# A graph network's second edge sort, run in one stage with the first layer's weighted sum and node update

## What is computed

```python
attn = attn_exp / (attn_sum[row] + 1e-08)
out = jax.ops.segment_sum(attn[:, :, None] * v[col], row, num_segments=n)
out = out.reshape(n, HID) @ Wo.T + bo
h = x + out
return layernorm(h) * ln_g + ln_b            # and then x = layernorm(x + that)
```

## Time and profile before

| | |
|---|---|
| median of 3 runs | 9654.35 us (9615.33 to 14809.4) |
| profiled execution, its own time | 9625.82 us |
| span of the profiled execution | 9624.1 us |
| sum0, from the softmax's end to the last addition | 2739 to 3056 us |
| update0 | 3056 to 3170 us |
| second sort | 3170 to 4351 us |
| POOL busy over the span | 6249.1 us (65%) |

### The profile page before, as it was taken

One profiled execution on the slowest core, in us unless ns is written; L12 is line 12 of the kernel. 1 busy time (PEld: TensorE's weight loads), 2 busy tenths in 40 slices (PEclk: granted clock), 3 DMA queues, 4 the chain that ended last, 5 costly groups with the idle time before them and its releaser, 6 DMA issues. The chain is left out here.

```text
span 9624.1 us, 137530 instructions
## 1 busy us (share of the span) xinstructions
PE 5695.4 (59%) x35183; PEld 5161.4 (54%) x35183; DVE 5182.6 (54%) x14594; ACT 2020.1 (21%) x3984; POOL 6249.1 (65%) x6325
## 2 busy tenths in 40 slices
PE   6777747777566576663777753777743333433334
PEld 5666637777545566663666643666633333333333
DVE  7666634444577655552777762444454444344445
ACT  0111111111156111111444432444430000000000
POOL 2777737777454577773777724777717777577774
PEclk9555568888778555557899975555555555655556
DMA  0000027777434000004555514334302111211111
GB/s 8 2 2 2 2 67 200 210 210 210 133 120 122 9 2 2 2 2 123 136 135 135 135 47 64 78 79 79 79 19 57 52 52 52 56 50 52 52 53 47
DMA packets 842488, 705.60 MB, mean 73 GB/s; under 512 B 308280, under 2 KB 733758, under 8 KB 841846
## 3 DMA queue, kind: packets, MB, share of 16 engines
q0 software_dynamic: 211680, 354.89, 15.2%
q1 hardware_dynamic: 499960, 286.30, 11.6%
q10 hardware_dynamic: 130584, 61.48, 2.2%
HBM read 608.13 MB, written 93.92 MB: 73 GB/s over the span
## 5 line engine op out<-in xcount | busy, mean ns | idle before, releaser
L1224 PE MATMUL sum_ps_sum<-sum_hot,sum_msg 128*128 128x128 f32 x3528 | 841.2, 431 | 1433.5 <-DVE acc L1193 1293.1
L1224 PEld LDWEIGHTS sum_ps_sum<-sum_hot,sum_msg 128*128 128x128 f32 x3528 | 770.5, 330 | 1504.3 <-DVE acc L1193 1348.1
L1292 POOL DMA_INDIRECT attend_rows<-h_table,dst_other x882 | 879.1, 997 | 521.5 <-issue 267.7
L1168 POOL DMA_INDIRECT sum_rows<-x_table,dst_other x882 | 845.5, 959 | 475.7 <-issue 268.5
L440 POOL DMA_INDIRECT payload_dst<-load_dst_pay_slot,load_dst_at_i x882 | 862.5, 978 | 440.4 <-issue 262.4
L440 POOL DMA_INDIRECT payload_src<-load_src_pay_slot,load_src_at_i x882 | 862.4, 978 | 438.1 <-issue 275.9
L1292 POOL DMA_INDIRECT attend_rows<-xl_table,dst_other x882 | 883.6, 1002 | 392.9 <-issue 268.6
L869 POOL DMA_INDIRECT scores_rows<-kv_table,scores_idx x882 | 833.7, 945 | 416.5 <-issue 254.7
L1168 POOL DMA_INDIRECT sum_rows<-conv_table,dst_other x882 | 843.8, 957 | 349.4 <-issue 268.5
L1364 PE MATMUL attend_ps_sum<-attend_hot,attend_msg 128*128 128x128 f32 x3528 | 669.2, 365 | 496.4 <-DVE acc L1525 496.4
L1364 PEld LDWEIGHTS attend_ps_sum<-attend_hot,attend_msg 128*128 128x128 f32 x3528 | 615.7, 270 | 540.4 <-issue 467.2
(11 more groups left out here) (461 smaller groups left out, 14731.6 us busy)
## 6 DMA issues: line engine op xcount, KB each, us to landing
attend_win<-xr_table SPq DMA_DIRECT2D x882, 68.0 KB
scores_win<-q_table ACTq DMA_DIRECT2D x882, 64.0 KB
spill<-scores_rows SPq DMA_DIRECT2D x126, 448.0 KB
sum_rows<-spill SPq DMA_DIRECT2D x126, 448.0 KB
attend_rel_all<-rel_flat_dst SPq DMA_DIRECT2D x252, 224.0 KB
payload_src<-load_src_pay_slot,load_src_at_i POOLq DMA_INDIRECT x882
scores_rows<-kv_table,scores_idx POOLq DMA_INDIRECT x882
payload_dst<-load_dst_pay_slot,load_dst_at_i POOLq DMA_INDIRECT x882
```

The costliest lines, as they stand in the source:

```text
L1168: pool.indirect_dma_start(rows[:, g % deep, j, :], None, table, bass.IndirectOffsetOnAxis(ap=o.other[:, t:t + 1].bitcast(U32), axis=0)).th ...
L1224: mm = pe.matmul(ps_sum[:, n, j, :], msg[:, n, j, :], hot[:, n, j, :], start=True, stop=True)
L1292: pool.indirect_dma_start(rows[:, g % RING, j, :], None, table, bass.IndirectOffsetOnAxis(ap=o.other[:, t:t + 1].bitcast(U32), axis=0)).th ...
```

## The change

The first sort keeps its code. The second sort, sum0 and update0 become one stage, `sort_and_sum`. What it does:

- It works in slots n = -1 to 129. In slot n, group n+1 is compared, spread and counted, group n is looked up, and group n-1 is placed.
- **Wide histograms.** The running table is no longer a chain through ACT. Seven matmuls (`tables`) write counts for all seven tiles at once into a table of 8 x 50 columns: tile j is added into all later columns, 350, 300, ... 50 wide. DVE adds the base once (`add_tables`), and PE does the seven look-ups in a row.
- **Ranks on ACT.** PE puts (key of the other edge, or 16384 more for later edges) in PSUM; ACT takes Square(key - own key) and then Relu(1 - that) with a running sum, tile by tile: 14 activations a group, and ACT also copies the turned one-hot out.
- **Ticks.** The 128 ticks of the weighted sum are spread over slots 3 to 97 (`LAST_SUM = 97`), one or two in each: 33 slots have two. A tick adds the last group's products to `acc`, multiplies the next rows by the weights, now on DVE, and makes the next one-hot. There is one accumulator and one PSUM tile `ps_sum` of 7 results (and `ps_d` has one buffer of 4 tiles). From slot 99 on, every second slot holds one block of the node update, which ends in slot 121.
- POOL does nothing in the stage but scatter. All 882 addresses and payloads have a place of their own, so POOL waits only for the group's addresses.
- The source order's per-edge buffers are freed before this stage. `rows_by_tile` follows as before.

The core of the new stage, the orders of the engines and what the steps wait for:

```diff
+        LAST_SUM = 97
+        n_slots = R + 4
+        ticks_by = lambda n: min(R + 2, max(0, (n - 2) * (R + 2) // (LAST_SUM - 2)))
+        sum_ticks = {n: [t - 1 for t in range(ticks_by(n - 1), ticks_by(n))] for n in range(-1, n_slots)}
+        norm_ticks = {LAST_SUM + 2 + 2 * m: m for m in range(blocks + 2)}
...
+            @block.gpsimd
+            def _(pool):
+                for t in range(T):
+                    if t % G == 0:
+                        pool.wait_ge(at_ready, t // G + 1)
+                    pool.indirect_dma_start(
+                        o.payload, bass.IndirectOffsetOnAxis(ap=at_i[:, t:t + 1].bitcast(U32), axis=0),
+                        pay[:, t, :], None).then_inc(scattered, 16)
...
+            @block.tensor
+            def _(pe):
+                def spread_keys(g):
+                    pe.wait_ge(row_in[g % 3], 16 * (g // 3 + 1))
+                    if g:
+                        pe.wait_ge(ranked, G * g)
+                    for g0, g1 in ((0, 4), (4, G)):
+                        out = ps_key[:, g0:g1, :]
+                        pe.matmul(out, c.ident_bf[:], per_tile(later_mask[:], g1 - g0), start=True, stop=False)
+                        mm = pe.matmul(out, two_ones[:], row2[:, g % 3, g0 * P:g1 * P].rearrange("k (g e) -> k g e", e=P),
+                                       start=False, stop=True)
...
+                def turn_low(g):
+                    pe.wait_ge(compared, 2 * (g + 1))
...
+                        mm = pe.transpose(ps_lo_t[:, j, :], lo3[:, g % 3, :, j], c.ident_bf[:])
...
+                def tables(g):
+                    if g:
+                        pe.wait_ge(tabled, g)
...
+                    for j in range(G):
+                        later = ps_tab[:, (j + 1) * HB:(G + 1) * HB].rearrange("p (n h) -> p n h", h=HB)
+                        mm = pe.matmul(later, lo3[:, g % 3, :, j],
+                                       hi3[:, g % 3, :, j].rearrange("p (o h) -> p o h", o=1).to_broadcast([P, G - j, HB]),
+                                       start=(j == 0), stop=True, skip_group_check=True)
+                    mm.then_inc(tallied, 1)
...
+                def fill(w, half):
...
+                    if w or half:
+                        pe.wait_ge(squared, 2 * w + half)
...
+                def sums(w):
+                    pe.wait_ge(hot_ready, w + 1)
+                    pe.wait_ge(msg_ready, w + 1)
+                    pe.wait_ge(added, 1 + G * w)
+                    for j in range(G):
+                        mm = pe.matmul(ps_sum[:, j, :], msg[:, w % 2, j, :], hot[:, w % 2, j, :], start=True, stop=True)
+                    mm.then_inc(summed, 1)
...
+                def sum_tick(t):
+                    if t + 1 < R:
+                        fill(t + 1, 0)
+                    if 0 <= t < R:
+                        sums(t)
+                    if t + 1 < R:
+                        fill(t + 1, 1)
...
+                for n in range(-1, n_slots):
+                    ticks = sum_ticks[n]
+                    if ticks:
+                        sum_tick(ticks[0])
+                    if n + 1 < R:
+                        spread_keys(n + 1)
+                        turn_low(n + 1)
+                    for t in ticks[1:]:
+                        sum_tick(t)
+                    if 0 <= n < R:
+                        look_up(n)
+                    if n + 1 < R:
+                        tables(n + 1)
...
+            @block.scalar
+            def _(act):
+                def ranks(g):
+                    act.wait_ge(keys_spread, g + 1)
...
+                    for j in range(G):
+                        t = g * G + j
+                        act.activation(same[:, j, :], ps_key[:, j, :], ACT.Square,
+                                       bias=minus_key[:, t:t + 1]).then_inc(squares, 1)
+                    act.wait_ge(squares, G * (g + 1))
+                    for j in range(G):
+                        act.activation(same[:, j, :], same[:, j, :], ACT.Relu, bias=c.ones[:, 0:1], scale=-1.0,
+                                       accum_out=rank[:, g % 3, j:j + 1]).then_inc(ranked, 1)
...
+                for n in range(-1, n_slots):
+                    ticks = sum_ticks[n]
+                    for t in ticks[:1]:
+                        if t + 1 < R:
+                            one_hot(t + 1)
+                    if n + 1 < R:
+                        low_back(n + 1)
+                        ranks(n + 1)
+                    for t in ticks[1:]:
+                        if t + 1 < R:
+                            one_hot(t + 1)
...
+            @block.vector
+            def _(dve):
...
+                def add_tables(g):
+                    dve.wait_ge(tallied, g + 1)
...
+                def additions(w):
...
+                    dve.wait_ge(summed, w + 1)
+                    for j in range(G):
+                        dve.wait_ge(added, 1 + w * G + j)
+                        to = acc[:, bass.ds(base[j], P)]
+                        dve.tensor_tensor(to, to, ps_sum[:, j, :], ALU.add).then_inc(added, 1)
+
+                def sum_tick(t):
+                    if 0 <= t - 1 < R:
+                        additions(t - 1)
+                    if t + 1 < R:
+                        message(t + 1)
...
+                for n in range(-1, n_slots):
+                    ticks = sum_ticks[n]
+                    if 0 <= n < R:
+                        add_tables(n)
+                    if 0 <= n - 1 < R:
+                        place(n - 1)
+                    for t in ticks[:1]:
+                        sum_tick(t)
+                    if 2 <= n + 2 < R:
+                        compare(n + 2)
+                    for t in ticks[1:]:
+                        sum_tick(t)
+                    if n in norm_ticks:
+                        norm_tick(norm_ticks[n])
...
@@ gnn_kernel
-            weighted_sum(nc, c, by_src, "sum0", acc, scores, H0, spill=spill)
-            node_update(nc, c, "update0", acc, x, "attend",
-                        {"w": wo_t[:], "b": bo[:], "g": ln_g[:], "be": ln_b[:]})
-
-        sort_edges(nc, c, by_dst, dst, src, edge_weight, real, dst_counts, True)
+            sort_and_sum(nc, c, by_dst, dst, src, edge_weight, real, dst_counts, by_src, scores, spill, acc, x,
+                         {"w": wo_t[:], "b": bo[:], "g": ln_g[:], "be": ln_b[:]})
+        rows_by_tile(nc, c, by_dst)
```

More of the change, by code:

```diff
@@ L125, with __init__ @@
 class Order:
-    def __init__(self, nc, name, keep, by_tile):
+    def __init__(self, nc, name, keep, edges, by_tile):
         self.name, self.by_tile = name, by_tile
@@ L230, in sort_edges @@
         totals = st.sb("totals", [P, HB])
-        if count_next is not None:
+        if True:
             next_lo, next_hi = st.sb("next_lo", [P, T], BF16), st.sb("next_hi", [P, T], BF16)
@@ L257, in _ @@
                 act.wait_ge(paid, 4)
-                if not counted_before:
+                if True:
                     act.wait_ge(counted, 1)
@@ L2051, in gnn_kernel @@
         dram = lambda n, s: nc.dram_tensor(n, s, F32).ap()
-        by_dst = Order(nc, "dst", keep, True)
+        by_dst = Order(nc, "dst", keep, keep, True)
         c = constants(nc, keep)
@@ L2088, in gnn_kernel @@
-            segment_softmax(nc, c, by_src, "softmax0", scores, H0,
-                            {"real": by_src.real[:], "cut": cut[:], "be2": be2}, acc)
-            weighted_sum(nc, c, by_src, "sum0", acc, scores, H0, spill=spill)
-            node_update(nc, c, "update0", acc, x, "attend",
-                        {"w": wo_t[:], "b": bo[:], "g": ln_g[:], "be": ln_b[:]})
-        sort_edges(nc, c, by_dst, dst, src, edge_weight, real, dst_counts, True)
+            wo_t, bo, ln_g, ln_b = (lsb(n, [P, D]) for n in ("wo_t", "bo", "ln_g", "ln_b"))
```

326 lines of the change are left out of this document (294 added, 32 removed).

## The result

The changed kernel takes 10,202.6 us (median; 10,199.5 to 10,207.0), the kernel before beside it 9658.7 us: a ratio of 1.058 (95% interval 1.054 to 1.061); one of the four executions of the kernel before, a slow one of 14,809 us, is left out of the ratio. It is slower, as forecast, but by twice the amount: 9900 was expected, and 10,203 lies just outside the range that ended at 10,150.

What follows compares the result with a forecast made beforehand. Old sort bound by POOL's issue, new ticked slots by DVE and PE taking turns: 53 + 1555 + 256 + 19 = 1883 us against 1612, +271 on 9625.8, say 9900 us; range 9600 to 10,150.

Steps and rivals of the forecast that it cites:

- The loop between DVE and PE: Joint stage's ticked slots: DVE's first part and PE's whole slot take turns; one-tick slot 13.7 us.
- Rival 1: Joint stage: the loop doesn't bind, POOL's scatters do; 425 us less, 9200 us; chance 0.10.
- DVE's part: Each ticked slot: placing, table addition, register loads and seven additions on one accumulator; 5.7 us.
- PE's part: Each ticked slot: sums, look-up, spreading, turning, tables, half a fill; 6.0 us at 2.4 GHz, 10.85 at 1.2 GHz.
- The clock: PE's burst in each slot starts at 1.2 GHz and rises 5 us in; together 7.9 us.
- rival 3: Joint stage: the clock never rises; slots 16.5 and 23.5 us, +515 us, 10,140 us; chance 0.16.
- Slots with two ticks: 33 of 95 slots: PE's second fill waits for ACT's square behind the ranks; 21.4 us each.
- Head and tail: Joint stage outside the ticked slots: 53 us to slot 3; behind slot 97, 256 us bound by POOL, then 19.
- Rival 4: Joint stage: DVE's two-input operations block POOL's issue, 0.2 us each, 41 us in all; 9940 us; chance 0.05.
- Rival 2: Joint stage: the loop binds, the clock stays high; slots 11.7 and 17.4 us, +15 us, 9640 us; chance 0.26.
- A rounding: Old second sort: 882 scatters at 1.26 us of POOL's issue, given as a floor of 1113 us.

Runs made afterwards that it cites:

- c3: Changed kernel with no weighted sum before the sort has ended, sums and then node update in slots behind it; 10,048 us, scatters 1155 us.
- e6: Changed kernel in its own order, with the one-hot high parts laid out tile by tile so the tables' streamed columns lie side by side; 9986 us, ratio 1.036.
- c1: The changed kernel as it is, repeated as the control; 10,191 us, scatters 2120 us.
- c4: Changed kernel with ScalarE's ranks behind both one-hot tiles of a slot; 10,087 us, ratio 1.046.
- e7: Changed kernel with TensorE's sort work ahead of its sums, sums over 113 slots, an update step in each later slot, high parts by tile; 9345 us.
- e4: The same kernel as c3, sort first and sums behind it, run on a slower chip; 12,589 us, scatters 1388 us.

## Why the prediction was right in its sign and short in its size

- *The loop between DVE and PE*: right. PE waits for `acc` once a slot, DVE for the tables once a slot, and the order alone, changed, gives 615 us back. Rival 1 (POOL binds) fell for the kernel as written, and c3 shows that it holds for the sort without the sums.
- *DVE's part, 5.7 us*: right, 5.7 measured: 2.78 from `add_tables` to the first addition, with 0.85 of idle time for the register loads in it (0.8), and 2.81 for seven additions (2.75).
- *PE's part*: `sums` 3.33, `look_up` 3.2, `turn_low` 0.95 and the fills as forecast or within 0.15. `spread_keys` took 1.94 at half clock (3511.01 to 3512.95) for 1.5. **`tables` took 2.38 for 1.4 at half and 2.36 for 0.8 at the full clock.** This is one of the two steps that failed: I had priced columns, 1400 of them, and not where they lie. e6 with the columns side by side has 1.37 and 0.79, my two numbers.
- *The clock*: the other step that failed. I let every burst turn to the full clock 5 us in. Some do (in c1 after 4.4 us), but in 44 of the 62 single slots the clock stayed at half to the end, and 43 slots took 17.5 us or more (in c1 3517.27 to 3534.75), which is rival 3's 16.5 and the 1.0 of the tables. The 17 slots in which the clock rose took 15.2 to 15.6, and the 1.5 that they lie above the forecast of 13.7 is the tables at the full clock (2.36 for 0.8). With 16.7 on average the single slots cost 62 x 3.0 = 186 us more than forecast, about half of it the tables and half the clock.
- *Slots with two ticks*: right in the mechanism (PE waits 2.31 us for a square behind the ranks; c4 takes it away), 23.8 us for 21.4. The ranks took 4.66 us (3514.74 to 3519.4; Squares 0.25 to 0.26 from start to start, Relu and read 0.39) for 4.2, the tables 1.0 more; the rest, 0.9, is put down to the clock, in 14 of the 33 at half throughout. 33 x 2.4 = 79 us.
- *Head and tail*: 63 us for 53, and 306 for 275. Behind slot 97 POOL was not quite the bound: the starts of line 764 lie 10.0 us apart, where I had 8.83 and POOL's own pace in c3 is 9.17. That is 10 of the 31 us; for the rest POOL waited, while the update's steps and the placing were in DVE's one queue.
- Sum: 186 + 79 + 10 + 31 = 306 us, and 303 were missed. Rival 4 is there but small: a scatter takes 1042 ns on average in the changed kernel, 984 in c3 and 978 before (862.5 / 882), 56 us in all, most of it where POOL idles anyway.
- *Rival 2 and 3*: the clock went to rival 3's side; its price, 10,140, lacked the tables, so the range ended 53 us short. e6, where the tables have the price that I gave them, took 9986 us, within the range; that kernel also had more of the full clock. The rule of the Trainium skill on bursts ("TensorE: Matmul & The Clock Gate", "HAM oscillation — how this bites in real kernels"), by which each burst begins cold, was the nearer one: with bursts of 9.5 to 18 us behind waits of some 5.2 us the mean clock of two stretches of 800 us was 0.53 and 0.56.
- *A rounding*: 882 x 1.26 is 1111 us, not 1113; nothing hangs on it.

## What to carry to other kernels

When two loops are joined slot by slot, write down which engine's last item of a slot the other's first item waits for. If each engine ends on what the other starts with, they take turns, and the joined loop is at least as long as the sum of the two (here 16.7 us for a single slot, against 8.6 for the sort's and 6.4 for the sum's in c3, and the program longer by 143 us than with one after the other); put the work that waits for nobody ahead of the work that waits, on each queue. And price a matmul's streamed operand by its layout as well as by its columns.

## What the runs showed of the hardware that was not expected

- A bf16 product of 128 partitions whose streamed columns lie 7 elements apart took 1.7 ns a column at either clock (2.37 us for 1400); side by side 0.98 ns at half and 0.56 at full, with the products' start-up in both.
- PE was busy 372 of 400 us in c3's sort, and the granted clock was 0.50 throughout; in e7 it was busy 357 of 400 and the clock 0.74. In this kernel a busy PE is no sign of a full clock:

```profile
2850.00:3250.00 400.00, 372.30 (x1495) 231.12 (x1496) 131.58 (x278) 257.49 (x1023) 298.95 (x305) 0.50 0.04 3
```

- On the slower chip e4 had stalls that the same kernel didn't have in c3, some 350 us in all: VectorE began `add_tables` some 5 us after the tables' end (3.5 to 7.7 in most cases), in about half of the slots. The profile names a transfer of the edge scores, long over by then, as what it waited for (idle time before the group, first e4, then c3). What held it up stays open:

```profile
L764 DVE TENSOR_TENSOR place_dst_tab<-place_dst_ps_tab,place_dst_tab 128x400 f32<-128x400 f32 x125 | 71.8, 575 | 1014.7 <-DMA spill<-scores_rows 684.2 <-PE place_dst_ps_tab L630 234.9 <-issue 95.6
```

```profile
L764 DVE TENSOR_TENSOR place_dst_tab<-place_dst_ps_tab,place_dst_tab 128x400 f32<-128x400 f32 x125 | 71.9, 575 | 709.5 <-PE place_dst_ps_tab L630 709.5
```
